# Half-width level products, dropped flushes and five stages on ScalarE in a chunked delta-rule attention layer

## The reference, cut to what matters

```python
def step(St, inp):
    qt, kt, vt, gt, bt = inp
    St = St * jnp.exp(gt)[..., None]
    err = jnp.einsum('bhk,bhkv->bhv', kt, St)
    St = St + bt[..., None, None] * kt[..., None] * (vt - err)[..., None, :]
    ot = jnp.einsum('bhk,bhkv->bhv', qt, St)
    return (St, ot)
_, o = jax.lax.scan(step, S0, (qs, ks_, vs, gs, bs))
```

## Time and profile before

| what | value |
|---|---|
| median of 3 runs | 10980.36 us (10976.84 to 10985.16) |
| the profiled execution's own time | 10982.68 us |
| its span | 10980.9 us |
| TensorE busy, matmuls | 10144.1 us, 92% |
| VectorE busy | 8773.9 us, 80% |
| ScalarE busy | 5870.0 us, 53% |
| GpSimd busy | 4217.7 us, 38% |
| mean granted TensorE clock | 0.975 of full speed |

### The profile page before, as it was taken

How to read it: one execution, slowest core, us unless ns; L and a number is a source line. 1 busy time by engine, 2 the same in 40 slices (tenths; PEclk the granted TensorE clock), 3 DMA queues, 4 the chain that set the end, 5 groups by cost and what they waited for, 6 DMA issues and landing times. The chain is left out here.

```text
span 10980.9 us, 274194 instructions
## 1 busy us (share of the span) xinstructions
PE 10144.1 (92%) x89648; PEld 7268.0 (66%) x89648; DVE 8773.9 (80%) x16670; ACT 5870.0 (53%) x12191; POOL 4217.7 (38%) x6737
## 2 busy tenths in 40 slices
PE   4899999999999999999999999999999999997888
PEld 1577767777677777776777777777777777774333
DVE  2788888888888888888888888888888888884111
ACT  1555555555555555555555555555555555553121
POOL 0344444444444444444444444444444444441000
PEclk7999999999999999999999999999999999998989
DMA  1111111111111111111111111111111111111000
GB/s 36 39 31 31 33 30 31 32 32 30 32 32 31 34 30 31 33 32 30 32 32 31 34 30 31 34 31 30 33 32 30 32 32 31 34 31 37 8 8 11
DMA packets 512026, 332.24 MB, mean 30 GB/s; under 512 B 63056, under 2 KB 509904, under 8 KB 511968
## 3 DMA queue, kind: packets, MB, share of 16 engines
q1 hardware_dynamic: 510912, 327.66, 11.4%
q0 software_dynamic: 1088, 4.26, 0.1%
HBM read 289.28 MB, written 42.47 MB: 30 GB/s over the span
## 5 line engine op out<-in xcount | busy, mean ns | idle before, releaser
L1124 POOL TENSOR_TENSOR KB<-KB,tot 128x256 f32<-128x256 f32 x1547 | 1271.5, 822 | 2912.5 <-PE bank L588 2910.7
L553 PE MATMUL bank<-hn,w_qkv 128*128 (+1 forms) x3108 | 1576.3, 631 | 403.2 <-DMA w_qkv<-in_L_attn_wq_dram 395.8
L1200 DVE SCALAR_TENSOR_TENSOR acc<-bank,hp,acc 128x510 f32<-128x510 f32 (+2 forms) x2331 | 1736.5, 745 | 92.2 <-ACT hnew L857 20.8
L588 PE MATMUL bank<-QKF,KB 128*128 128x128 f32 x12376 | 1728.8, 282 | 36.5 <-DVE QKF L1279 31.7
L588 PEld LDWEIGHTS bank<-QKF,KB 128*128 128x128 f32 x12376 | 1525.6, 191 | 248.4 <-issue 185.6
L1261 DVE COPY_PREDICATED BIG<-masks,bank 128x512 f32<-128x512 int32 x1290 | 1228.5, 952 | 123.0 <-DVE BIG L1244 72.9
L1273 DVE TENSOR_TENSOR QKF<-QKF,tot 128x512 f32<-128x512 f32 x1547 | 1165.2, 753 | 121.8 <-PE bank L588 82.4
L632 PEld LDWEIGHTS bank<-invT,Zm 64*64 64x64 f32 x20592 | 704.3, 135 | 827.4 <-issue 796.4
L1279 DVE TENSOR_SCALAR QKF<-QKF 128x512 f32<-128x512 f32 x1804 | 1180.0, 666 | 8.8
L553 PEld LDWEIGHTS bank<-hn,w_qkv 128*128 128x128 f32 x3108 | 537.0, 192 | 869.3 <-issue 830.3
L856 ACT ACTIVATE acc<-bank,hp 128x512 f32<-128x512 f32 x777 | 533.9, 687 | 885.2 <-PE bank L553 864.2
(11 more groups left out here) (202 smaller groups left out, 19504.7 us busy)
## 6 DMA issues: line engine op xcount, KB each, us to landing
bb<-beta_rows SPq DMA_DIRECT2D x518, 128.0 KB, 3.9
states<-StC SPq DMA_DIRECT2D x288, 128.0 KB, 2.4
w_qkv<-in_L_attn_wk_dram SPq DMA_DIRECT2D x260, 128.0 KB, 2.2
w_qkv<-in_L_attn_wv_dram SPq DMA_DIRECT2D x260, 128.0 KB, 2.1
w_qkv<-in_L_attn_wq_dram SPq DMA_DIRECT2D x259, 128.0 KB, 3.8
StA<-states SPq DMA_DIRECT2D x258, 128.0 KB, 2.1
w_o<-in_L_attn_wo_dram SPq DMA_DIRECT2D x256, 128.0 KB, 2.2
w_fb<-in_L_attn_f_b_dram SPq DMA_DIRECT2D x260, 64.0 KB, 4.0
```

What stands on the lines that cost most here:

```text
L553: mm = eng.matmul(rows(BK["proj_" + "qkv"[n_]]), w_qkv[:, n_, k, :], hn_v[:, k, :, cols], start=(k == 0), stop=(k == KD - 1))
L588: mm = eng.matmul(ps[:, :, ch, :, :], kb[:, ch, :], QKF[par][:, :, ch, :].rearrange("p f (n two m) -> p f n two m", two=2, m=m)[:, :, :, 1 ...
L1124: eng.tensor_tensor(e_, e_, t_.to_broadcast([P, C, P // (2 * m), m]), ALU.mult).then_inc(ev[f"kb_mul{s}"], 1)
L1200: eng.scalar_tensor_tensor(dst, rows(bk)[:, :, 0:BLK - sh], hp[par][:, w_:w_ + 1], dst, ALU.mult, ALU.add).then_inc(ev[("tap_" if t_ < 2 e ...
```

## The change

TensorE: `diag` and levels 0 to 5 are two matmuls for each chunk, each of 64 weight columns and 64 moving columns (diagonal: 64 and 64), written to partitions 0 to 63 and 64 to 127. Level 6 takes 64 weight columns and 128 moving ones. The flushes `round_keys` (levels 0 to 6) and `round_qk` of levels 3 to 6 are gone. On ScalarE now: the copy of level 4 (four pieces), the copy of odd keys, the last growth of keys and of queries (four instructions each), and the rounding of 1 + u in softplus. `softplus_low` goes from GpSimd to VectorE as one instruction; the diagonal's product with the identity is a masked copy. The orders of all five engines and the table of banks are new.

```diff
                         eng.wait_ge(ev["kk_mul"], done(j))
                         eng.wait_ge(ev["silu_qk"], done(j))
+                        eng.sem_inc(waited, 1)
                         for ch in range(C):
-                            mm = eng.matmul(chains(BK["diag"])[:, ch, :], kk[:, ch, :], q_[:, ch, :], start=True, stop=True)
+                            for h in range(2):
+                                rw = slice(h * HALF, (h + 1) * HALF)
+                                mm = eng.matmul(chains(BK["diag"])[rw, ch, rw], kk[:, ch, rw], q_[:, ch, rw], start=True, stop=True)
                         mm.then_inc(ev["diag_mm"], 1)
 
...
                     def level(s, j, par):
@@ -580,14 +584,23 @@
                             eng.wait_ge(ev["qk_init"], done(j))
                             eng.wait_ge(ev["kk_mul"], done(j))
                         else:
-                            eng.wait_ge(ev[f"kb_up{s - 1}"], done(j))
+                            eng.wait_ge(ev[f"kb_mul{s - 1}"], done(j))
                             eng.wait_ge(ev[f"qk_up{s - 1}"], done(j))
+                            if s == 1:
+                                eng.wait_ge(ev["kb_odd"], done(j))
+                        eng.sem_inc(waited, 1)
                         m = 1 << s
                         ps = bank[BK[f"lvl{s}"]][:, :].rearrange("p (f c n m) -> p f c n m", f=2, c=C, m=m)
-                        for ch in range(C):
-                            mm = eng.matmul(ps[:, :, ch, :, :], kb[:, ch, :],
-                                            QKF[par][:, :, ch, :].rearrange("p f (n two m) -> p f n two m", two=2, m=m)[:, :, :, 1, :],
-                                            start=True, stop=True)
+                        if s == LEVELS - 1:
+                            for ch in range(C):
+                                mm = eng.matmul(ps[0:HALF, :, ch, :, :], kb[:, ch, 0:HALF], QKF[par][:, :, ch, HALF:], start=True, stop=True)
+                        else:
+                            for ch in range(C):
+                                for h in range(2):
+                                    rw = slice(h * HALF, (h + 1) * HALF)
+                                    mm = eng.matmul(ps[rw, :, ch, h * (QUART // m):(h + 1) * (QUART // m), :], kb[:, ch, rw],
+                                                    QKF[par][:, :, ch, rw].rearrange("p f (n two m) -> p f n two m", two=2, m=m)[:, :, :, 1, :],
+                                                    start=True, stop=True)
                         mm.then_inc(ev[f"lvl_mm{s}"], 1)
 
                     def first_inverse(j):
@@ -681,7 +694,7 @@
                         mm.then_inc(ev["O_mm"], 1)
 
...
                     def step(i, par):
-                        if on(i + 2):
-                            load_state(i + 2, par, i)
-                        if on(i):
-                            load_wo(i)
+                        if on(i + 1):
+                            load_gb(i + 1)
+                        if on(i + 4):
+                            load_fb(i + 4)
                         if on(i + 4):
                             load_w(1, i + 4)
-                        if on(i + 1):
-                            load_gb(i + 1)
-                        if on(i + 3):
-                            load_beta(i + 3)
                         if on(i + 4):
-                            load_fb(i + 4)
-                        if on(i + 3):
-                            load_w(0, i + 3)
+                            load_w(0, i + 4)
+                        if on(i + 4):
+                            load_w(2, i + 4)
+                        if on(i + 1):
+                            load_wo(i + 1)
+                        if on(i + 3):
+                            load_state(i + 3, 1 - par, i)
                         if on(i):
                             store_state(i)
                         if on(i + 4):
-                            load_w(2, i + 4)
+                            load_beta(i + 4)
 
                     loop(eng, step)
...
+                    def take_level(s, j, pj):
+                        eng.wait_ge(ev[f"lvl_mm{s}"], done(j))
+                        eng.wait_ge(ev[f"z_mm{s}"], free(j))
+                        eng.wait_ge(ev["O_mm"], free(j, 2))
+                        eng.wait_ge(ev["lvl_e3"], done(j))
+                        m = 1 << s
+                        dst = big(s, pj)
+                        ps = bank[BK[f"lvl{s}"]][:, :].rearrange("p (f c n) -> p f c n", f=2, c=C)
+                        for n_ in range(P // (2 * m)):
+                            lo = n_ * 2 * m
+                            x_ = eng.activation(dst[lo:lo + m, :, :, lo + m:lo + 2 * m], ps[lo:lo + m, :, :, n_ * m:(n_ + 1) * m], ACT.Copy)
+                        x_.then_inc(ev[f"lvl_e{s}"], 1)
 
...
+                    def softplus_round(f):
+                        eng.wait_ge(ev["u_exp"], done(f))
+                        eng.wait_ge(ev["a_exp"], free(f))
+                        eng.activation(r[:, :, :], u[:, :, :], ACT.Identity, bias=1.0).then_inc(ev["r_rnd"], 1)
+
                     def softplus_log(f):
-                        eng.wait_ge(ev["u_exp"], done(f))
-                        eng.activation(zc[:, :, :], u[:, :, :], ACT.Ln, bias=1.0).then_inc(ev["ln_w"], 1)
+                        eng.wait_ge(ev["r_rnd"], done(f))
+                        eng.wait_ge(ev["z_clip"], done(f))
+                        eng.activation(zc[:, :, :], r[:, :, :], ACT.Ln).then_inc(ev["ln_w"], 1)
+
+                    def copy_odd_keys(j):
+                        eng.wait_ge(ev["kk_mul"], done(j))
+                        eng.wait_ge(ev["kb_tr"], free(j))
+                        eng.activation(blocks(KB[:, :, :], 0)[:, :, :, 1, :], blocks(kk[:, :, :], 0)[:, :, :, 1, :], ACT.Copy).then_inc(ev["kb_odd"], 1)
+
+                    def grow_last_qk(j, pj):
+                        eng.wait_ge(ev["lvl_mm6"], done(j))
+                        eng.wait_ge(ev["tots"], done(j))
+                        for ch in range(C):
+                            x_ = eng.activation(QKF[pj][:, :, ch, HALF:], QKF[pj][:, :, ch, HALF:], ACT.Copy, scale=tot[6][:, ch, 0:1])
+                        x_.then_inc(ev["qk_up6"], 1)
+
+                    def grow_last_keys(j):
+                        eng.wait_ge(ev["lvl_mm6"], done(j))
+                        eng.wait_ge(ev["tots"], done(j))
+                        for ch in range(C):
+                            x_ = eng.activation(KB[:, ch, 0:HALF], KB[:, ch, 0:HALF], ACT.Copy, scale=tot[6][:, ch, 1:2])
+                        x_.then_inc(ev["kb_mul6"], 1)
 
...
-                        eng.sem_inc(waited, 1)
-                        eng.tensor_copy(blocks(KB[:, :, :], 0)[:, :, :, 1, :], blocks(kk[:, :, :], 0)[:, :, :, 1, :])
...
-                        eng.wait_ge(ev[f"kb_up{s - 1}"], done(j))
+                        eng.wait_ge(ev[f"kb_mul{s - 1}"], done(j))
+                        if s == 1:
+                            eng.wait_ge(ev["kb_odd"], done(j))
...
-                    def round_w(f):
-                        eng.wait_ge(ev["u_exp"], done(f))
-                        eng.wait_ge(ev["a_exp"], free(f))
-                        eng.tensor_scalar(r[:, :, :], u[:, :, :], 1.0, -1.0, ALU.add, ALU.add).then_inc(ev["r_rnd"], 1)
+                    def softplus_low(f):
+                        eng.wait_ge(ev["r_rnd"], done(f))
+                        eng.scalar_tensor_tensor(u[:, :, :], r[:, :, :], -1.0, u[:, :, :], ALU.add, ALU.subtract).then_inc(ev["u_minus_r"], 1)
...
-                        eng.tensor_tensor(qkT[pj], chains(BK["diag"]), identb, ALU.mult).then_inc(ev["diag_cp"], 1)
+                        eng.sem_inc(waited, 1)
+                        eng.copy_predicated(qkT[pj], ident[:, :].bitcast(I32).unsqueeze(1).to_broadcast([P, C, P]),
+                                            chains(BK["diag"])).then_inc(ev["diag_cp"], 1)
...
-                        eng.tensor_tensor(o_, o_, t_.unsqueeze(1).to_broadcast([P, 2, C * P // (2 * m), m]), ALU.mult).then_inc(ev["qk_mul"], 1)
+                        eng.tensor_tensor(o_, o_, t_.unsqueeze(1).to_broadcast([P, 2, C * P // (2 * m), m]), ALU.mult).then_inc(ev["qk_mul" if s < ROUNDED else f"qk_up{s}"], 1)
...
-                    def round_keys(s, j):
-                        eng.wait_ge(ev[f"kb_mul{s}"], done(j))
-                        e_ = blocks(KB[:, :, :], s)[:, :, :, 0, :]
-                        eng.tensor_scalar(e_, e_, ROUND, -ROUND, ALU.add, ALU.add).then_inc(ev[f"kb_up{s}"], 1)
```

More of the change, by code:

```diff
@@ L735, in step @@
                         if on(i + 2):
                             level(0, i + 2, par)
-                        read(eng, "z_cp4", i + 1)
+                        read(eng, "lvl_e6", i + 1)
+                        if on(i + 3):
+                            project(0, i + 3)
+                        read(eng, "St_up1", i)
+                        if on(i + 1):
```

(44 more changed lines are left out.)

346 lines of the change are left out of this document (148 added, 198 removed).

## The result

The changed kernel takes 10901.99 us (median of 5 runs, 10878.19 to 10929.09) against 10980.36 us of the kernel before (5 runs, 10976.18 to 10995.32): a ratio of 0.9927, 95% interval 0.9903 to 0.9951. The forecast of 10180 us, and its range, missed it. The profiled execution spans 10877.7 us.

The account below looks back on a forecast made before the run. TensorE was taken as the bound, with the q weights' wait added: 35.5 - 2.9 + 1.0 = 33.6 us of work plus 0.7 VectorE wait, 34.3 a step against 37.4, giving 10180 us (range 9860 to 10540).

Parts of the forecast that it names:

- the four rivals: Forecast, 0.70; another engine's chain paces it, 0.18, 10540 us; halves take turns, 0.06, 10850; slower, 0.05, 12390.
- The step: One loop step: 33.6 us of TensorE work plus 0.7 waiting for VectorE, 34.3 against 37.4 before.
- Halves side by side: Diagonal, levels 0 to 5: paired half-width products overlap, 0.47 us a level, 2.9 saved a step; chance 0.70.
- The third rival: Half-width level products take turns instead of overlapping, VectorE's wait vanishes: 10850 us; chance 0.06.
- the fourth: Weights of one half can't load while the other multiplies: 1.8 us a level, 12390 us; chance 0.05.
- Changes of shape: TensorE switching between wide and narrow groups: 3.5 us a step before, 4.6 after, 1.0 given back.
- The q weights: TensorE's wait for wq to land, 1.5 us a step, goes whole because wq is issued earlier.
- VectorE's chain before the turn of level 5: VectorE's work through level 5's subtraction makes TensorE wait between 0 and 0.9 us a step, taken as 0.7.
- ScalarE: Gains some 4 us on 22, leaving 0.3 to 0.5 us slack at three places; nothing charged.
- Outside the loop: Time outside the loop does not change.

Follow-up runs that it names:

- The second experiment: The kernel before with its level and diagonal products in two column blocks of 64, order, flushes and ScalarE stages unchanged: 11234.39 us, ratio 1.0234.

## Why the prediction was wrong

**The step that failed** is the first one, and it is unspoken: TensorE's time was taken as its products, its changes of shape, and its waits for data of other engines and of DMA. I counted sixteen instructions in place of eight for their duration and never for their number. Doubling them made the loop body outgrow what TensorE holds, and a fifth source of waiting, its own program, came in. None of the four rivals was this one. It costs 10902 - 10094 = 808 us, which is more than all of the miss: with the same loop 120 records further on, the kernel takes 10094 us, 86 below the forecast. Between the two profiled executions the difference is 786 us, and two parts make it up. TensorE's idle time in the loop is 735 us against 158. These 577 are the gaps, 606 with those before L715, less some 29 of other waits that they take the place of. The other 209 are the same instructions taking longer behind the gaps, at the lower clock: 2.2 us for each of the 93 (1.97 us for the level-6 group after a gap, 1.09 in the run below).

The Trainium skill names the mechanism (Runtime: NRT & Kernel Launch, Instruction fetch mechanics): an engine's instruction store is refilled in blocks of 16 KiB, 256 instructions, TensorE's holds 2,048, and a taken branch whose target is not in the current window of two pages has to fetch before it can go on. The runs agree with the block (248 records to a packet) and with the kind of wait. They agree with neither size: two pages would have the kernel before fetch in every pass, and it has 13 packets in all; 2,048 would hold 1,729 records wherever they begin, and they stay only where seven blocks, 1,792 records, cover them. The measurement decides. The likely reason for seven is that the block behind the branch is fetched ahead and takes the place of the first one. Nine packets to a pass fit that, since the body touches eight blocks ((852 - 13) / 93 here, (1158 - 13) / 127 in the run with 10 matmuls); it was not tried by itself.

The rest of the steps, read in the run with 30 throw-away matmuls, whose loop is that of the changed kernel undisturbed. First the window of the earlier trace rows and the transpose of the earlier trace rows:

```profile
4000.00:6000.00 2000.00, 1963.55 (x23336) 1397.14 (x23335) 1639.40 (x2946) 1508.61 (x3530) 816.63 (x1356) 1.00 0.14 35
```

```profile
L701 PE MATMUL bank<-ident,KB x1028: 272/273/273, 352.3 to 9049.7; 128*128 128x128 f32 x172
```

**The step**: (9049.4 - 352.3) / 256 = 33.97 us, forecast 34.3; within a block of heads it is 33.8. Of the 3.44 us won against the kernel before, 1.06 are idle time (429 us in the loop before, 158 here; forecast 0.8, the wait for the weights less the new one) and 2.38 are work (forecast 2.3, the blocks and the clock less the changes of shape). So the nearness to the forecast comes from its parts and not from luck, though two small misses in the work offset each other: 0.71 came with the order (forecast 0.4) and 1.67 with the blocks (forecast 1.9).

**Halves side by side**: right. Full width in the new order, then column blocks at the same place in the order:

```profile
4020.05 0.60 PE L663 MATMUL bank<-ident,invT 128*128 128x128 f32 x4
4020.49 1.06 PE L601 MATMUL bank<-QKF,KB 128*128 128x128 f32 x8
4021.38 0.61 PE L685 MATMUL bank<-R,invT 128*128 128x128 f32 x4
4021.92 0.66 PE L638 MATMUL bank<-invE,BIG 64*64 64x32 f32 x16
...
4025.07 1.16 PE L601 MATMUL bank<-QKF,KB 128*128 128x128 f32 x8
4026.07 1.06 PE L578 MATMUL bank<-qk,kk 128*128 128x128 f32 x8
4026.96 0.60 PE L663 MATMUL bank<-ident,invT 128*128 128x128 f32 x4
```

```profile
4009.65 0.60 PE L655 MATMUL bank<-ident,invT 128*128 128x128 f32 x4
4010.18 0.69 PE L603 MATMUL bank<-QKF,KB 128*64 128x64 f32 x16
4010.79 0.71 PE L677 MATMUL bank<-R,invT 128*128 128x128 f32 x4
4011.43 0.66 PE L630 MATMUL bank<-invE,BIG 64*64 64x32 f32 x16
...
4014.59 0.69 PE L603 MATMUL bank<-QKF,KB 128*64 128x64 f32 x16
4015.10 0.64 PE L580 MATMUL bank<-qk,kk 128*64 128x64 f32 x16
4015.67 0.66 PE L655 MATMUL bank<-ident,invT 128*128 128x128 f32 x4
```

From start to start a level between wide groups takes 0.89 at full width and 0.61 in column blocks; a level and the diagonal in a row take 1.00 + 0.89 and 0.51 + 0.57. That is the 0.47 and its border of the forecast. The third rival (halves in turn) and the fourth (weights in the open) have nothing for them. The Trainium skill's rule that the fourth leaned on (TensorE: Matmul & The Clock Gate, Part 3), that a load overlaps only with matmuls of another row group, does not show here: both halves use all rows, and sixteen products take 0.51 us.

**Changes of shape**: right in kind and near in size. The wide groups beside a block grow, as from 0.54 (4021.38 to 4021.92) to 0.64 (4010.79 to 4011.43). A full-width kernel steps at 35.13 us (its transposes from 348.4 to 9342.3), so all column blocks together are worth 1.16 us a step, 3%. TensorE idles for only 27 us in that kernel's loop, 0.10 a step, against 0.62 here. So its work fell by 1.67 us a step, where the forecast had 2.9 - 1.0 = 1.9, and 0.52 of that went to the two waits named below, which the full width does not have.

**The q weights**: right, the wait is gone whole. With the flushes and the order it is what carries the change: 37.4 to 35.1 us a step at full width, of which 1.5 are that wait; the flushes, the ScalarE stages and the order were not tried one by one. The second experiment is the other half of it, since with the old order the blocks gain nothing.

**VectorE's chain before the turn of level 5**: right in place and releaser, too long. Forecast 0.7, measured 75.2 us in 255 times, 0.3 each, in the waits of that run (from start to start the projection before the turn takes 0.45 more than at full width); the one below it was not forecast:

```profile
PE bank L655 <- DVE invT L1351: 75.2, 255, 2.0
...
PE bank L685 <- issue: 60.9, 263, 0.3
```

**ScalarE**: charged at nothing, cost 0.24. The state products L685 need ScalarE's copy of U, and that stood behind a table load and the logarithm of softplus (L975):

```profile
4003.52 1.28 ACT L1076 ACT_TABLE_LOAD   x1
4004.81 0.63 ACT L975 ACTIVATE zc<-r 128x512 f32<-128x512 f32 x1
4005.35 0.36 ACT L909 ACTIVATE U<-bank 128x256 f32<-128x256 f32 x1
```

The copy ends at 4005.71 and TensorE's group starts at 4005.81, after 0.24 idle. That it is the copy is read from these times, not tried. The slack I had laid out for the copy was before `outputs`; it went first before the state products.

**Outside the loop**: right, 1,395 us in that run and 1,402 before.

## What to carry to other kernels

Count an edit's instructions as well as their time: TensorE held a loop's body here only where seven blocks of 256 cover it, and an fp32 matmul in the code is four instructions. (The other engines' limits were not tried.) The page tells it at once, in the packets of the queue named "instruction": a dozen means that the loop is held, hundreds mean that it is fetched. What that costs stands at the branch, as idle time with the releaser "issue"; the body of sixteen steps had 902 packets and lost little. Mend it by a shorter body, by one that branches back less often, or by where it begins; a body near the limit changes by 9% in time with what stands ahead of it, so two versions of a kernel are only compared rightly when both are held.

## What was not expected of the hardware

- After a branch back to code that is not held, TensorE stood still for 6.7 us in the mean in the changed kernel, 5.1 us in the same with 10 matmuls ahead (616 us in 120 gaps), and 2.7 us in the old order with padding (329 in 120). In all of these gaps TensorE starts again 1.8 to 2.8 us after a packet of its program has landed. What differs is when that packet is sent, counted from TensorE's last work: 2.3 and 2.2 us after it in the first two (medians), 1.0 before it in the old order; and in the changed kernel it takes 2.1 us to land, against 1.0 in the second. Why it is sent when it is stays open.
- A body with eight blocks is not fetched in every pass. In the run with 55 matmuls passes of 67.6 us without a packet and passes with nine take turns:

```profile
q1 hardware_dynamic: 3642, 2.36, 12.7%
q8 instruction: 9, 0.15, 0.9%
```

  The share grew with the distance past the room (583, 852, 1158 packets for the changed loop), but the padded old order fetched in every pass at a distance where the changed loop did so in half. Nor did one kernel always do the same: the run with levels 3 and 4 at full width and 30 matmuls took 10472 to 11293 us. What decides between them wasn't found.
- The gap is followed by about 10 us with the clock at 1.2 GHz or between the levels: a pause costs its length and some 2 us more, though passes of the same kernel differ (75 to 81 us, against 67.7 without a pause).
- Sixteen products of 64 columns on all 128 rows, two and two on halves of the columns, run at 0.51 us for sixteen where the next group has the same shape.
